# Order of the triangle's matmuls, order of the last block's loads, and high rows shared by two blocks

## What is computed

```python
zn, pp, lp, ip = ...                                  # layer-normed grids, [b, i, k, 128]
gate_proj = lambda x, Wg, bg, W, b: sigmoid(x @ Wg + bg) * (x @ W + b)      # 128 -> 64 channels
ab1, ab2, ab3 = (gate_proj(zn, ...) * zm for each of three weight sets)
pp, lp, ip = gate_proj(pp, ...), gate_proj(lp, ...), gate_proj(ip, ...)
block = einsum('bikc,bkjc->bijc', pp, ab1) + einsum('bikc,bjkc->bijc', ab2, lp) + ab3 * ip
out = sigmoid(zn @ Wend + bend) * (layernorm(block) @ Wsum + bsum) * zm
```

## Time and profile before

| | us |
|---|---|
| median of 3 runs (lowest, highest) | 1477.86 (1474.34, 1480.62) |
| the profiled execution | 1476.01 |
| its span on the core | 1474.3 |
| projection | 0 to 565 |
| border (nothing on PE) | 564 to 575 |
| triangle | 575 to 724 |
| mix and routing | 725 to 949 |
| feed-forward | 950 to 1474 |

### The profile page before, as it was taken

How to read it: one execution, slowest core, us unless ns; L and a number is a source line. 1 busy time by engine, 2 the same in 40 slices (tenths; PEclk the granted TensorE clock), 3 DMA queues, 4 the chain that set the end, 5 groups by cost and what they waited for, 6 DMA issues and landing times. The chain is left out here.

```text
span 1474.3 us, 32179 instructions
## 1 busy us (share of the span) xinstructions
PE 1361.6 (92%) x9869; PEld 1134.6 (77%) x9869; DVE 1225.5 (83%) x4155; ACT 983.9 (67%) x2293; POOL 1007.1 (68%) x1555
## 2 busy tenths in 40 slices
PE   5999999999999986899789999499999999999993
PEld 2877778877778865788666666389999999999983
DVE  6998999998999863677699999567888888888996
ACT  3888888888888864344367777246677676776763
POOL 3999999999999984445378888324555555555663
PEclk9999999999999998999999999799999999999997
DMA  9999999999999978989689996211222322232222
GB/s 212 209 261 247 261 237 256 244 258 254 255 244 249 244 191 258 282 273 289 181 254 299 297 299 198 104 30 44 86 72 72 87 72 87 72 85 74 73 57 72
DMA packets 358375, 270.63 MB, mean 184 GB/s; under 512 B 60710, under 2 KB 333054, under 8 KB 358206
## 3 DMA queue, kind: packets, MB, share of 16 engines
q1 hardware_dynamic: 356924, 268.16, 69.4%
q10 hardware_dynamic: 1010, 0.20, 0.1%
q0 software_dynamic: 272, 0.21, 0.1%
HBM read 174.16 MB, written 94.37 MB: 182 GB/s over the span
## 5 line engine op out<-in xcount | busy, mean ns | idle before, releaser
L1467 ACT ACTIVATE hT<-psH_d,b 128x512 f32<-128x512 f32 x288 | 198.0, 688 | 162.6 <-PE psH_d L1502 162.4
L1489 PE MATMUL psY_d<-w,hT 128*128 128x128 f32 x2304 | 268.9, 275 | 0.0
L1489 PEld LDWEIGHTS psY_d<-w,hT 128*128 128x128 f32 x2304 | 263.0, 192 | 0.1
L642 PE MATMUL psZ_a<-w_all,xT_a 128*128 128x128 f32 x1728 | 232.0, 278 | 4.9 <-DVE low_pp L717 4.9
L642 PE MATMUL psZ_a<-w_all,xT_block 128*128 128x384 f32 x576 | 214.6, 496 | 8.4 <-DVE low_ab L711 5.5
L642 PEld LDWEIGHTS psZ_a<-w_all,xT_a 128*128 128x128 f32 x1728 | 211.9, 193 | 7.5 <-issue 5.1
L566 ACT ACTIVATE sig_a<-psZ_a 128x256 f32<-128x256 f32 (+1 forms) x360 | 153.4, 426 | 88.1 <-PE psZ_a L642 51.2
L578 POOL TENSOR_SCALAR shared<-shared,coefs_early 128x128 f32<-128x128 f32 x468 | 203.2, 449 | 0.0
L629 PE MATMUL psT_a<-ident,shared 128*128 128x128 f32 x1152 | 187.0, 275 | 3.4 <-issue 2.0
L629 PEld LDWEIGHTS psT_a<-ident,shared 128*128 128x128 f32 x1152 | 142.1, 142 | 54.3 <-issue 27.7
L1526 POOL TENSOR_TENSOR u_d<-u_d,gamma 128x512 f32<-128x512 f32 x72 | 96.0, 1333 | 124.9 <-ACT u_d L1453 109.6
(11 more groups left out here) (218 smaller groups left out, 2940.7 us busy)
## 6 DMA issues: line engine op xcount, KB each, us to landing
shared<-in_x_dram SPq DMA_DIRECT2D x48, 512.0 KB, 5.7
scratch_xT<-xT_block SPq DMA_DIRECT2D x36, 512.0 KB, 5.3
shared<-scratch_xT SPq DMA_DIRECT2D x36, 512.0 KB, 5.0
scratch_x<-x_c SPq DMA_DIRECT2D x36, 512.0 KB, 4.2
shared<-scratch_x SPq DMA_DIRECT2D x36, 512.0 KB, 3.6
shared<-in_x_dram SPq DMA_DIRECT2D x48, 256.0 KB, 5.2
shared<-L_conv_protein_pair_dram SPq DMA_DIRECT2D x24, 512.0 KB, 7.6
shared<-in_L_conv_l_pair_dram SPq DMA_DIRECT2D x24, 512.0 KB, 8.9
```

The source lines that it names most:

```text
L642: ins = nc.tensor.matmul(out, turned_x(G, i, t0, size)[:, j * P:j * P + P], rhs[i], start=True, stop=True)
L1467: nc.scalar.activation(hT[:, S % 2, f, :], psH[:, f, :], ACT.Gelu, bias=s["b1"][:, f:f + 1]).then_inc(gelued, 1)
L1489: ins = nc.tensor.matmul(psY[:, G % 2, i * CH:i * CH + CH], hT[:, G % 2, f, i * P:i * P + P], s["w2"][:, f, :], start=(f == 0), stop=(f == ...
```

## The change

1. In the triangle PE does the three wide matmuls of both channels of a pair, then the half-width matmuls of both, then `turn(Q + 1)`.
2. SP's list for the last block is written by hand (`last_body`): the turned x and the last pp and lp of the block before are stored as in other blocks, the operand loads come behind them, and the late columns of a tensor are loaded as soon as its own stores have landed, so that only two DMAs stand behind the last lp store.
3. The scratch tiles of the setup lie in `xT_block`, which frees the room for number 4; the mask is copied in four DVE instructions in place of two.
4. High rows: blocks 2m and 2m + 1 share 32 rows of the grid; partition half h holds rows 32m + 16h and up, the even block the first 8 of the 16, the odd block the other 8 (`high_from`). Both blocks' products lie side by side in `high_ab`, `high_pp`, `high_lp`, and are stored by the odd block only, in runs of 16 rows x 8 channels (512 B) in place of 8 x 8 (256 B). Low and high stores have semaphores of their own. In the triangle the half-width matmuls pick their columns by the new map.

```diff
@@ -64,6 +65,11 @@
         self.eng.wait_ge(self.sem, self.count)
 
 
+def high_from(n, h):
+
+    return 2 * BLOCK_A * (n // 2) + BLOCK_A * h + HALF_A * (n % 2)
+
+
 def load_tiles(eng, dst, src, n, sem, tiles=(0, TPB)):
 
     lo, hi = tiles
...
@@ -73,7 +79,7 @@
     if hi > LOW:
         for h in range(2):
             eng.dma_start(dst[64 * h:64 * h + 64, LOW:TPB, :],
-                          src[bass.ds(BLOCK_A * n + HALF_A * h, HALF_A), P:N, :].rearrange("a b c -> b a c")
+                          src[bass.ds(high_from(n, h), HALF_A), P:N, :].rearrange("a b c -> b a c")
                           ).then_inc(sem, 16)
 
 
...
@@ -453,11 +461,17 @@
 
         @block.sync
         def _(sp):
-            def load_operands(names, a_lo, a_hi):
+            def load_operands(names, late):
 
                 for name in names:
-                    for dst, src in operand_loads(s["operands"], d, name, 0, a_lo, a_hi):
+                    edge = N - BLOCK_A * (1 + name.endswith("high"))
+                    for dst, src in operand_loads(s["operands"], d, name, 0, *((edge, N) if late else (0, edge))):
                         sp.dma_start(dst, src).then_inc(s["operands_loaded"][0], 16)
+
+            def all_stored(i, blocks):
+
+                sp.wait_ge(stored_low[i], 16 * blocks)
+                sp.wait_ge(stored_high[i], 32 * (blocks // 2))
 
             def load_third(i, k, n):
                 load_tiles(sp, tiles_in[i], srcs[i], n, loaded[i][k], CHUNKS[k])
@@ -468,10 +482,10 @@
                     sp.wait_ge(multiplied, NG_A * n + PASS_END[i])
                     dst, groups = (d["s_ab"], d["s_pp"], d["s_lp"])[i], (2 * NCG, NCG, NCG)[i]
                     sp.dma_start(dst[0:P, :, bass.ds(CC * BLOCK_A * n, CC * BLOCK_A)],
-                                 low_out[i][:, 0:groups, :]).then_inc(stored[i], 16)
-                    for h in range(2):
-                        sp.dma_start(dst[P:N, :, bass.ds(CC * BLOCK_A * n + CC * HALF_A * h, CC * HALF_A)],
-                                     high_out[i][64 * h:64 * h + 64, 0:groups, :]).then_inc(stored[i], 16)
+                                 low_out[i][:, 0:groups, :]).then_inc(stored_low[i], 16)
+                    for h in range(2 * (n % 2)):
+                        sp.dma_start(dst[P:N, :, bass.ds(CC * high_from(n - 1, h), 2 * CC * HALF_A)],
+                                     high_out[i][64 * h:64 * h + 64, 0:groups, :]).then_inc(stored_high[i], 16)
 
             def store_xT(n, k):
 
...
-                            sp.wait_ge(turned, NG_A * n + PASS_START[i] + CHUNKS[k][1] // PASSES[i][2])
-                            load_third(i, k, n + 1)
-                            if i == 0:
-                                store_xT(n, k)
-                                if n > 0 and k < 2:
-                                    store_out(n - 1, k + 1)
-                    else:
-
-                        sp.wait_ge(turned, NG_A * n + PASS_END[i])
-                        sp.wait_ge(stored[min(i, 2)], 48 * n)
-                        load_operands(OPERANDS[2 * i:2 * i + 2], 0, N - BLOCK_A)
+                    for k in range(len(CHUNKS)):
+
+                        sp.wait_ge(turned, NG_A * n + PASS_START[i] + CHUNKS[k][1] // PASSES[i][2])
+                        load_third(i, k, n + 1)
                         if i == 0:
-                            for k in range(len(CHUNKS)):
-                                store_xT(n, k)
-                                if k < 2:
-                                    store_out(n - 1, k + 1)
-                        if last and i > 0:
-                            store_out(n, i)
+                            store_xT(n, k)
+                            if n > 0 and k < 2:
+                                store_out(n - 1, k + 1)
                     if i == 0:
                         store_out(n, 0)
-            for n in range(NBLK):
-                body(n, n == NBLK - 1)
+
+            def last_body(n):
+
+                of_ab, of_pp, of_lp = (("ab1_high", "ab1_low", "ab2_low"), ("pp_low", "mov_high"), ("lp_low",))
+                for k in range(len(CHUNKS)):
+                    sp.wait_ge(turned, NG_A * n + PASS_START[0] + CHUNKS[k][1] // PASSES[0][2])
+                    store_xT(n, k)
+                    if k < 2:
+                        store_out(n - 1, k + 1)
+                all_stored(0, n)
+                load_operands(OPERANDS[0:2], False)
+                store_out(n, 0)
+                for i in range(1, 3):
+                    sp.wait_ge(turned, NG_A * n + PASS_END[i])
+                    all_stored(i, n)
+                    load_operands(OPERANDS[2 * i:2 * i + 2], False)
+                    store_out(n, i)
+                all_stored(0, NBLK)
+                load_operands(of_ab, True)
+                all_stored(1, NBLK)
+                load_operands(of_pp, True)
+                sp.wait_ge(turned, NG_A * n + PASS_START[3] + STA_GROUPS)
+                load_operands(OPERANDS[6:], False)
+                all_stored(2, NBLK)
+                load_operands(of_lp + OPERANDS[6:], True)
+
+            for n in range(NBLK - 1):
+                body(n)
+            last_body(NBLK - 1)
             for k in range(len(CHUNKS)):
                 sp.wait_ge(stored_xT[k], 16 * NBLK)
-            for i in range(3):
-                sp.wait_ge(stored[i], 48 * NBLK)
-            load_operands(OPERANDS, N - BLOCK_A, N)
-
 
         def norm(wait, engine_op, sem_out, n, G, which, last):
 
...
@@ -696,13 +720,15 @@
                     else:
                         dve.wait_ge(gated, NG_A * n + G + 1)
                     if g == 0 and i < 3:
-                        need(dve, stored[i], 48 * n)
+                        need(dve, stored_low[i], 16 * n)
+                    if t0 == LOW and i < 3:
+                        need(dve, stored_high[i], 32 * (n // 2))
                     if i == 0 and g % 2 == 0:
                         need(dve, q_made, QG * (n - 1) + g // 2 + 1)
                     if i == 3:
                         need(dve, q_made, QG * n + g - 3)
                     if i < 3:
-                        buf, a, t = (low_out[i], LOW, t0) if t0 < LOW else (high_out[i], HIGH, t0 - LOW)
+                        buf, a, t = (low_out[i], LOW, t0) if t0 < LOW else (high_out[i], 2 * HIGH, HIGH * (n % 2) + t0 - LOW)
                         out = buf[:].rearrange("p g (a c) -> p g a c", a=a)[:, :, t:t + size, :].rearrange("p g a c -> p a g c")
                     gate = sig[:, G % 2, :]
                     if i == 0:
...
                     ins = nc.tensor.transpose(ends(half), row(par, "ab1_high", a, 2 * q), ident[:])
                 ins.then_inc(turned, 1)
 
+            def sides(Q, e):
+
+                return [(sta[:, Q % 2, e, :], mov[:, Q % 2, e, :]) for sta, mov in ((ab1T, pp_now), (lp_now, ab2_now), (sta_now, mov_now))]
+
             turn(0)
-            for C in range(HID):
-                Q, e = divmod(C, 2)
-                if e == 0:
-                    pe.wait_ge(copied, Q + 1)
-                    pe.wait_ge(packed_act, Q + 1)
-                    pe.wait_ge(packed_pool, Q + 1)
-                    pe.wait_ge(packed_dve, Q + 1)
-                need(pe, taken, 2 * (C - 3))
-                out = psO[:, C % 4, :]
-                steps = [(sta[:, Q % 2, e, :], mov[:, Q % 2, e, :]) for sta, mov in ((ab1T, pp_now), (lp_now, ab2_now), (sta_now, mov_now))]
-                for k, (sta, mov) in enumerate(steps):
-                    nc.tensor.matmul(out[:, 0:N], sta[:, 0:P], mov, start=(k == 0), stop=(k == 2))
-                for k, (sta, mov) in enumerate(steps):
-                    for h in range(2):
-                        part = mov.rearrange("p (n u) -> p n u", u=LOW)[:, :, HIGH * h:HIGH * h + HIGH]
-                        ins = nc.tensor.matmul(out[64 * h:64 * h + 64, N:N + N // 2], sta[:, P:N], part,
-                                               start=(k == 0), stop=(k == 2))
-                ins.then_inc(summed, 1)
-                if e == 0 and Q + 1 < PAIRS_B:
+            for Q in range(PAIRS_B):
+                pe.wait_ge(copied, Q + 1)
+                pe.wait_ge(packed_act, Q + 1)
+                pe.wait_ge(packed_pool, Q + 1)
+                pe.wait_ge(packed_dve, Q + 1)
+                for e in range(2):
+                    C = 2 * Q + e
+                    need(pe, taken, 2 * (C - 3))
+                    for k, (sta, mov) in enumerate(sides(Q, e)):
+                        nc.tensor.matmul(psO[:, C % 4, 0:N], sta[:, 0:P], mov, start=(k == 0), stop=(k == 2))
+                for e in range(2):
+                    C = 2 * Q + e
+                    for k, (sta, mov) in enumerate(sides(Q, e)):
+                        for h in range(2):
+                            ins = nc.tensor.matmul(psO[64 * h:64 * h + 64, C % 4, N:N + N // 2], sta[:, P:N], high_half(mov, h),
+                                                   start=(k == 0), stop=(k == 2))
```

(11 more changed lines are left out.)

29 lines of the change are left out of this document (13 added, 16 removed).

## The result

The changed kernel takes 1495.99 us (median of 4 runs, 1494.61 to 1498.30) against 1477.86 before: 1.0128 times as long (95% interval 1.0106 to 1.0150), 18.1 us slower. Forecast were 1491 us and, between the two profiled executions, +12.9; they are 1476.01 and 1496.58, +20.6.

What follows compares the result with a forecast made beforehand. It took PE to bound the triangle, loads close behind, and a border of waits in front: triangle +23.4 and border -10.5 gave +12.9 us, 1488.9 against the profiled execution, 1491 for the median, range 1481 to 1499.

Steps and rivals of the forecast that it cites:

- The triangle: Whole triangle: -10.9 for fewer switches, +39.7 for uncovered copies, -5.6 for load waits, +0.2 at the end: +23.4 us.
- the saving: PE within a triangle pair: one turn from wide to half-width and one back dropped, 0.34 us a pair, -10.9 us.
- the copies cost: Triangle, behind the transposes: PE waits uncovered for ACT's copies, 1.28 us more in 31 pairs, +39.7 us.
- the way from the end of the copy to PE: Triangle: from the end of ACT's copy to PE's next start, 0.23 us, read in the first pair.
- The 5.6 us: Triangle: PE's standing time, read as waits for a set's 9 loads at its start, would go: -5.6 us.
- the prediction's reading of 0.99: Triangle: the granted clock stayed 0.99 through stands at each set's start, held against a falling clock.
- The clock rival: Triangle: idle time in each pair lowers PE's clock; 1522 us for a quarter of the pairs, +120 for all; chance 0.06.
- The border (a): Last projection block: its stall, PE 8.3 us late, goes, so PE ends at 555.7.
- The border (b): Tail before the triangle: the queue drains 9.84 MB at 277 GB/s in 35.5 us; first copy at 564.4, -10.5 us.
- a first copy after 571: Start of the triangle: a sign that the forecast is wrong; the first copy was expected near 564.5.
- The rest, nothing: High stores in the projection, setup and column picking: no time won or lost, PE being the bound at 44.02 us a block.
- The border's -10.5: Between projection and triangle: the first copy comes at 564.4 in place of 574.95, -10.5 us.

Runs made afterwards that it cites:

- kernel 4: The changed kernel with the next pair's transposes moved between the two channels' wide matmuls: 1476.54 us.
- kernel 5: The changed kernel with the next pair's transposes between the wide and the half-width matmuls: 1473.10 us.
- 8: The changed kernel with the odd blocks' doubled high store of ab put in halves behind the reloads of pp and lp, last block unchanged: 1489.85 us.
- 9: The changed kernel with the high ab stores later and PE's order in the triangle as before the change: 1467.66 us.
- 3: The changed kernel without the sharing of high rows, each block storing its own in runs of 256 B: 1488.58 us.
- 2: The kernel before with only the new list of the last block, separate semaphores and the setup in `xT_block`: 1463.96 us.
- 6: The changed kernel without sharing of high rows and with the next pair's transposes between the two channels' wide matmuls: 1466.19 us.

## Why the prediction came out as it did

**The triangle: right in mechanism, 3.8 us too much.** Forecast +23.4, measured +19.6. A pair is 5.17 us (forecast 5.25). Against kernel 4 the saving is 0.35 a pair (forecast 0.34) and the copies cost 5.17 - 3.96 = 1.21 (forecast 1.28), so 37.5 us and not 39.7. But in the kernel after the transposes still stand behind a half-width matmul, and 0.10 of both numbers is theirs: there the saving is 0.25 and the copies cost 1.22 - 0.11 = 1.11. Both terms were too large, and the errors are of opposite sign. The step was the way from the end of the copy to PE, 0.23 us, read in the first pair, where the clock is at its lower level; in the kernel after PE starts 588.81 - (588.28 + 0.47) = 0.06 us behind it. That makes the whole way 1.22 us and not 1.39. Without the pairs themselves, 32 x (5.165 - 4.31) = +27.4, the triangle fell by 7.8 us where 5.4 were forecast: load waits, and what PE lost behind them. The 5.6 us that the prediction read as waits for loads were 4.4 by PE's waits; the rest is mostly the end of the stretch, where PE had finished. But the granted clock was at 0.50 for over 2 us behind one of these waits (1.85 us, to 615.48), which the prediction's reading of 0.99 hid, and that time came back too.

**The clock rival: wrong.** PE stands 0.94 us in each 5.17 and the granted clock is 1.00. The Trainium skill, TensorE: Matmul & The Clock Gate (A second HAM failure mode: psum-queue depth-cycling), tells of short idle times between groups that made the clock swing; this trace doesn't agree for stands of this length. The clock does fall behind some of the longer waits for loads: in the kernel before behind 1.85 us but not behind 2.02, in kernel 5 behind 3.28 us but not behind 3.61. What else decides it is open.

**The border (a): right.** The last block's 8.3 us are gone: block 10's store of ab is 7.14 us late, PE's end 1.14 early, 8.28 in all.

**The border (b): right in mechanism, too small in size, and in part right by luck.** The drain from the third xT store takes 573.98 - 536.86 = 37.1 us (forecast 35.5 and 0.5 for a wait), at 276 GB/s in the stretch above; in 8 and 9, which move the same 9.84 MB, it takes 37.5 and 36.8. Without sharing the triangle starts at 564.3 or 564.8 (kernels 3 and 2), where 564.4 was forecast; but there are 1.05 MB less to move, for which the prediction's own rate gives 31.7 us, and the drains take 35.1 and 34.8. So that hit is luck. With sharing and the later stores the start is 566.7. The prediction had named a first copy after 571 as a sign against it, and that is what came.

**"The rest, nothing": this is the step that failed.** It said that sharing buys no time in the projection, "since PE is the bound there" and that "the odd block's double store has a whole pass before its buffer is wanted". It asked when the buffer of the store is wanted, and not what is queued behind the store: the reloads of pp. Priced at 0, it cost 7.1 us in the projection, all of which experiment 8 took back (block 10 stores its ab at 489.05 there). The border's -10.5 became -1.0 by these 7.1, by 1.1 of the longer drain, and by 1.3 by which the drain starts late beyond that (536.86 against 528.4 + 7.1). That the error of +9.5 there and the one of -3.8 in the triangle partly cancel is luck, and it is why the median came within 5 us (between the two profiled executions, with the +1.9 of the stages behind, it is 7.7). The cost is of four blocks in which DVE waits up to 2.9 us; the store itself took no longer to issue than before (3.59 us for its two halves in block 3, 3.95 before).

**Of the sum,** in the order of the prediction: projection 0, measured +7.1; last stall -8.3, -8.3; tail -2.2 by its own (8.7 us against 10.98), +0.2; triangle +23.4, +19.6; the stages behind 0, +1.9. 12.9 and 20.6.

What stays open: why the tail is 11 us in both, to the parts. 1.05 MB at 276 GB/s is 3.8 us, and taking it away gave 2.5 at the triangle's start and 2 more within it. And whether packets of 256 B move slower than those of 512: the kernels with and without them differ in bytes at the border too (8.79 MB in 34.8 to 35.1 us, 9.84 MB in 36.8 to 37.5), a fixed part of the drain would give the same, and none was run that changes only the packets.

## What to carry to other kernels

When transposes and their copies go through another engine, what counts is the work between the last transpose and the first use: 1.1 us of half-width matmuls was as good as 2.2, and none cost 1.2 us in each of 31 pairs. Before an order is tuned to spare PE's switches, look whether the loads leave room: here PE and DMA were both full, and 11 us less of PE's work were worth nothing. A store that is made larger and rarer is priced by what its queue holds behind it and by where the last one falls (here 7.1 us and some 2 us), not by when its own buffer is wanted.

## What the runs showed of the hardware

- In a pair that has one group of half-width matmuls in place of two, and its transposes behind a wide matmul in place of a half-width one, PE takes 3.96 us in place of 4.31, with matmuls of 0.33 and 0.16 us: 0.25 us go with the switch from wide to half-width and back, 0.10 with the place of the transposes.
- Stands of 0.94 us every 5.17 us leave the clock at 1.00. Behind single waits for loads it fell to 0.50 for some us in one case and not in another: it fell behind 1.85, 2.28, 2.75 and 3.28 us, it stayed at 1.00 behind 2.02, 2.86, 3.05 and 3.61 us (kernels before, 4, 5 and 6). At 0.50 the same matmul takes 0.84 in place of 0.49 us.
- 24576 packets of 512 B in place of 49152 of 256 B gave no gain that could be seen: 1467.66 against 1463.96 us with the same order of PE, 1.05 MB more in the drain included, and blocks of the projection of 44.03 to 44.09 us with either (kernels 3 and 8).
